# One kernel, two moved places: the last step of the projection stage, and the order of the convolution, projection and feed-forward products

## The reference, cut to what matters

```python
xn = layernorm(x)
x = x + attn(xn) + ffn(xn)

def attn(x):
    proj = x @ in_proj_w + in_proj_b             # v, ctrl 1, ctrl 2
    v = proj[..., :d]
    for i in range(2):
        ctrl = proj[..., (i + 1) * d:(i + 2) * d]
        xc = conv3(ctrl)                          # three taps along the tokens, and a bias
        gate = sigmoid(xc @ gate_w[i] + gate_b[i])
        v = long_conv(v, filter_i) * (xc * gate)
    return v @ out_proj_w + out_proj_b

def ffn(x):
    h = x @ tern_fc.T + gate * low_rank(x)
    r = maximum(h, 0)
    return (r * r) @ tern_proj.T
```

## Time and profile before

| what | value |
| --- | --- |
| median of three runs | 844.11 us (843.82 to 844.96) |
| the profiled execution's own time | 846.87 us |
| its span in the trace | 845.3 us |
| mean granted TensorE clock | 0.994 of full speed |
| PE busy | 814.5 us (96%) |
| DVE, ACT, POOL busy | 604.0 us (71%), 542.2 us (64%), 195.5 us (23%) |
| setup and projection stage | to about 312 us |
| mixing stage | about 312 to 779 us |
| output projection | about 779 us to the end |

### The profile page before, as it was taken

The page is one execution under the profiler, slowest core; times in us unless marked ns, Lnnn a source line. Parts: engine busy times, 40 slices in busy tenths (PEclk is TensorE's granted clock), DMA queues, the critical chain, the costliest instruction groups (busy, mean ns, idle before and its releaser), DMA issues.

```text
span 845.3 us, 24948 instructions
## 1 busy us (share of the span) xinstructions
PE 814.5 (96%) x9280; PEld 684.4 (81%) x9281; DVE 604.0 (71%) x992; ACT 542.2 (64%) x861; POOL 195.5 (23%) x235
## 2 busy tenths in 40 slices
PE   7899999999999979999999999999999999999997
PEld 3588888888888757788888888888888888888997
DVE  7989899999899754556565656556646656667997
ACT  6989899989989854455555555544444444444773
POOL 4944565565565000000100011000000000100000
PEclk9999999999999989999999999999999999999999
DMA  8863423422421558688868788678888877951896
GB/s 227 236 235 123 177 101 109 188 100 103 182 113 74 168 189 188 145 176 164 196 154 185 156 183 200 143 160 190 192 143 182 185 178 131 220 109 43 223 320 232
DMA packets 90541, 141.99 MB, mean 168 GB/s; under 512 B 12845, under 2 KB 70590, under 8 KB 89470
## 3 DMA queue, kind: packets, MB, share of 16 engines
q1 hardware_dynamic: 72846, 101.80, 50.3%
q0 software_dynamic: 7728, 28.05, 10.4%
q10 hardware_dynamic: 9920, 11.54, 4.1%
HBM read 97.39 MB, written 43.97 MB: 167 GB/s over the span
## 4 chain that ended last, share of the span: by engine, by line
PE 53%; DVE 5%; issue 4%; DVEq 0%
PE pp L1451 15%; PE py L1470 14%; PE pf L1420 12%; PE pf L1426 3%; PE py L1438 2%; PE py L1510 2%; DVE pp L1200 2%; DVE GC L1210 1%; DVE xb L1210 1%; PE pp L467 1%; PE pp L469 1%; PE pp L468 1%; PE pf L467 1%; PE pf L468 1%; PE pf L469 1%
## 5 line engine op out<-in xcount | busy, mean ns | idle before, releaser
L1344 ACT ACTIVATE r_hi<-r 128x512 fp32r<-128x512 f32 x128 | 80.8, 632 | 126.3 <-DVE r L1215 126.3
L1339 ACT ACTIVATE r<-pf,fscale 128x512 f32<-128x512 f32 x128 | 88.0, 688 | 103.1 <-PE pf L1426 102.1
L1470 PEld LDWEIGHTS py<-vwin,lead 64*64 64x64 f32 x5120 | 133.6, 133 | 24.6 <-issue 24.6
L1470 PE MATMUL py<-vwin,lead 64*64 64x128 f32 (+4 forms) x5120 | 147.8, 266 | 1.1 <-issue 1.1
L1420 PE MATMUL pf<-tokens,split_a 128*128 (+1 forms) x512 | 139.5, 394 | 0.7 <-issue 0.7
L1451 PE MATMUL pp<-wproj,r_hi 128*128 128x256 f32 x512 | 134.7, 296 | 4.9 <-DVE GC L1210 1.8
L1220 DVE TENSOR_TENSOR r_lo<-r,r_hi 128x512 fp32r<-128x512 f32 x128 | 88.1, 689 | 67.2 <-ACT r_hi L1344 67.1
L1451 PE MATMUL pp<-wproj,r_lo 128*128 128x256 f32 x512 | 126.9, 281 | 1.1 <-issue 1.1
L1451 PEld LDWEIGHTS pp<-wproj,r_hi 128*128 128x128 f32 x512 | 96.2, 188 | 21.9 <-issue 8.7
L508 POOL TENSOR_SCALAR lead<-lead,norms 128x256 f32<-128x256 f32 x64 | 110.2, 1732 | 3.9 <-POOL norms L502 3.4
L705 DVE SCALAR_TENSOR_TENSOR xc<-ctrls,taps,xc 128x512 f32<-128x512 f32 x128 | 96.5, 792 | 17.9 <-ACT xc L806 17.0
(11 more groups left out here) (212 smaller groups left out, 1622.6 us busy)
## 6 DMA issues: line engine op xcount, KB each, us to landing
lead<-filters SPq DMA_DIRECT2D x128, 320.0 KB, 6.2
xnT_hbm<-split_b SPq DMA_DIRECT2D x30, 512.0 KB, 3.8
tokens<-xnT_hbm POOLq DMA_DIRECT2D x30, 512.0 KB, 4.7
lead<-in_attn_x SPq DMA_DIRECT2D x16, 512.0 KB, 3.9
gc_hbm<-xc SPq DMA_DIRECT2D x16, 512.0 KB, 2.6
GC<-gc_hbm SPq DMA_DIRECT2D x32, 256.0 KB, 6.2
out<-GC ACTq DMA_DIRECT2D x15, 512.0 KB, 7.4
GC<-in_attn_x POOLq DMA_DIRECT2D x9, 512.0 KB, 7.6
```

The source lines that it names most:

```text
L1339: act.activation(r[j][:, :], pf[:, j, :], ACT.Relu, scale=fscale[:, m:m + 1]).then_inc(relu_done, 1)
L1344: act.activation(r_hi[j][:, :], r[j][:, :], ACT.Copy).then_inc(r_hi_done, 1)
L1470: last = pe.matmul(py[g % 2][q * BW:(q + 1) * BW, side, l, :, A:NB], tile[rows, q * PAIR + l, j * BW:(j + 1) * BW], vwin[g % 2][rows, q, l ...
```

## The change

It has four parts, and line numbers in the changed file differ by up to 41.

1. In step 16 ACT follows a list of its own, `last_gates`: all four first taps, then all four roundings, then all four sigmoids. The rows 2 and 3 are written to the idle control buffer `ctrl[0]` in place of `xc`, and step 16 of ACT no longer waits for `gc2_saved`. DVE's order is as before, with the new buffer. SP stores from the new buffer.
2. In step 16 PE follows `last_gates(o)`: the high-part passes for each input half as soon as that half is rounded, then the passes with the low part. The products are the same 12. The products without use are five, not seven.
3. In the mixing stage `fc(it, 2 * g)` stands ahead of `proj(*late[0])` and gives `near_mm`.
4. ACT waits for `gc2_saved` before the loop of the mixing stage; POOL loads `srow` behind the first tokens and behind a wait for `gc2_saved`.

```diff
+        def second_gates(s0):
+            return ctrl[NCH % 2][:, KT:2 * KT, 0:CH] if s0 == NCH else xc[:, KT:2 * KT, :]
+        def mixed(c, s0):
+            return xc_blocks[:, :, c, :] if c < KT else blocks(second_gates(s0)[:, c - KT, :])
...
-                    sp.dma_start(gc2_hbm[bass.ds(s - 1, 1)]..., xc[:, KT:2 * KT, :]).then_inc(gc2_saved, 16)
+                    sp.dma_start(gc2_hbm[bass.ds(s - 1, 1)]..., second_gates(s0)).then_inc(gc2_saved, 16)
...
+                def last_gates():
+                    act.wait_ge(xc_ready, 4 * s)
+                    act.wait_ge(gcT_mm, s)
+                    for c in range(4):
+                        first_tap(c)
+                    act.wait_ge(gate_mm, 4 * s)
+                    for c in range(4):
+                        high(c)
+                    for c in range(4):
+                        sigmoid(c)
+                    act.wait_ge(gcT_mm, s + 1)
+                    transposed_gates()
...
+                def last_gates(o):
+                    def passes(co, k, w, x, start=False, stop=False):
+                        c, ws = KT * o + co, slice(co * P, (co + 1) * P)
+                        return pe.matmul(pc[:, c, :], Wgate[w][:, KT * o + k, ws], xcs[o][x][:, k, :], start=start, stop=stop)
+                    for k in range(KT):
+                        pe.wait_ge(xc_hi_done, 4 * s - 4 + KT * o + k + 1)
+                        for co in range(KT):
+                            if k == 0:
+                                pe.wait_ge(gc_done, 4 * s - 4 + KT * o + co + 1)
+                            passes(co, k, 0, 0, start=k == 0)
+                            passes(co, k, 1, 0)
+                    for k in range(KT):
+                        pe.wait_ge(xc_split, 4 * s - 4 + KT * o + k + 1)
+                        for co in range(KT):
+                            last = passes(co, k, 0, 1, stop=k == KT - 1)
+                            if k == KT - 1:
+                                last.then_inc(gate_mm, 1)
...
-                    for _ in range(7):
+                    for _ in range(5):
                         pe.matmul(pT[:, 0, :], ident[:, :], Wvs[:, 0, :, :]...)
...
             pool.dma_start(bo_row[:, :], ...).then_inc(bo_in, 16)
-            pool.dma_start(srow[:, :], ...).then_inc(srow_in, 16)
             pool.wait_ge(first_in, 32)
             pool.wait_ge(y_out, 3)
             load_xn(1, 1)
+            pool.wait_ge(gc2_saved, 16 * NCH + 16)
+            pool.dma_start(srow[:, :], ...).then_inc(srow_in, 16)
             load_xb(0, True)
...
             window(0, 0, 0, 0)
             rank_high(0)
+            act.wait_ge(gc2_saved, 16 * NCH + 16)
...
+                        fc(it, 2 * g, m % 2, near_mm)
                         if late:
-                            proj(*late[0], near_mm)
-                        fc(it, 2 * g, m % 2, None if late else near_mm)
+                            proj(*late[0])
```

More of the change, by code:

```diff
@@ L704, in tap @@
                         dve.wait_ge(before, 4 * s - 4 + c + 1)
-                        dve.scalar_tensor_tensor(out=mixed(c), in0=tapped(ctrl[1 - par], c, k_), scalar=kw[:, c, k_:k_ + 1],
-                                                 in1=mixed(c), op0=ALU.mult, op1=ALU.add).then_inc(done, 1)
+                        dve.scalar_tensor_tensor(out=mixed(c, s0), in0=tapped(ctrl[1 - par], c, k_), scalar=kw[:, c, k_:k_ + 1],
+                                                 in1=mixed(c, s0), op0=ALU.mult, op1=ALU.add).then_inc(done, 1)
                 def low(c):
@@ L805, in first_tap @@
                         act.wait_ge(halo_done, 4 * s - 4 + c + 1)
-                        act.activation(mixed(c), tapped(ctrl[1 - par], c, 0), ACT.Identity, bias=kb[:, c:c + 1],
+                        act.activation(mixed(c, s0), tapped(ctrl[1 - par], c, 0), ACT.Identity, bias=kb[:, c:c + 1],
                                        scale=kw[:, c, 0:1]).then_inc(tap0_done, 1)
@@ L832, in store_V, with transposed_gates @@
                     to_V(lambda out, rows: act.activation(out, rows, ACT.Copy), act, s, s0, parity)
+                def transposed_gates():
+                    pk = (s0 - 1) % 4
+                    act.activation(GC1[:, :, bass.ds(batch(act, s - 1, s0 - 1), 1), TB * pk:TB * pk + TB].rearrange("p c n a -> p c (n a)"),
+                                   pn[:, :, :].rearrange("p i c -> p c i"), ACT.Copy).then_inc(gc1_stored, 1)
+                def last_gates():
[10 more added lines that the diff above has]
+                    transposed_gates()
+                if s0 == NCH:
+                    last_gates()
+                    return
                 if back:
@@ L931, in gates @@
                         c = KT * o + co
-                        if front:
-                            pe.wait_ge(ctrl_copied, 4 * s + c + 1)
-                        else:
-                            pe.wait_ge(gc_done, 4 * s - 4 + c + 1)
+                        pe.wait_ge(ctrl_copied, 4 * s + c + 1)
                         for k in range(KT):
@@ L945, in step @@
                     pe.wait_ge(gcT_mm, NCH)
-                    for _ in range(7):
+                    for _ in range(5):
                         pe.matmul(pT[:, 0, :], ident[:, :], Wvs[:, 0, :, :].bitcast(F32).rearrange("p k c -> p (k c)"), start=True, stop=True)
                 if back:
-                    gates(0)
+                    (gates if front else last_gates)(0)
                 if ahead and s0:
@@ L952, in step @@
                 if back:
-                    gates(1)
+                    (gates if front else last_gates)(1)
                     pe.wait_ge(gc_done, 4 * s + KT)
@@ L1157, in _ @@
             load_xn(1, 1)
+            pool.wait_ge(gc2_saved, 16 * NCH + 16)
+            pool.dma_start(srow[:, :], bass.AP(scales.tensor, 0, [[0, P], [1, D]])).then_inc(srow_in, 16)
             load_xb(0, True)
```

15 lines of the change are left out of this document (5 added, 10 removed).

## The result

The changed kernel takes **840.35 us** (median of 7 runs, 838.07 to 843.29); the kernel before, run beside it, takes 844.43 us (7 runs, 843.71 to 847.13). The ratio is 0.9943, with a 95% interval of 0.9921 to 0.9965. So it is faster, by 4.1 us where 9.4 were forecast, and 1 us above the forecast range.

A forecast was written before the change was run, and what follows sets the result against it. PE, busy for 96% of the span, was taken to bound the kernel with its products and pauses. Border 4.8 us plus mixing order 4.6 us, 9.4 in all, off 844.11 gave 834.7 us; range 832.3 to 839.4.

The forecast's parts named there:

- Taps and store: Step 16: ACT's two more taps fit its idle time, without waiting for the store; DVE goes on 2.16 us sooner.
- High passes ahead: Step 16: PE starts eight high passes at the first rounding; the 12 products run at full clock, about 1.3 and 1.5 us.
- The border, 4.8 us: Border from projection to mixing stage moves 4.8 us: 2.16 from taps, about 1.3 from passes, about 1.5 from clock.
- The clock falls at the border: Assumed at the stages' border: after a pause of about 2.5 us the first convolution still runs slow, 3.43 us.
- The likeliest case: Whole kernel: the forecast comes out as told, 834.7 us; chance 44%.
- the clock stays up: Rival, 33%: full clock over the stages' border, first convolution 2.28 us; 1.6 us more gained, 833.1 us.
- The new waits for the store: ACT's and POOL's waits for the gates' store, ahead of their mixing-stage work, cost nothing.
- `fc` ahead of `proj`, 4.6 us: Mixing stage, group 1 of fifteen passes: `proj`'s waits on `add` go and none replace them; 4.6 us gained.
- The branch: Rival, 5%: the branch on a flag shows as a pause in each group; 0.3 us a group gives 854 us.
- The sum, 9.4 us: Whole kernel: 4.8 us from the border plus 4.6 us from the mixing stage, giving 834.7 us.
- The border gives half: Rival, 8%: clock falls before step 16's 12 products, which take 4.3 us again; 836.2 to 837 us.
- the mixing stage gives nothing: Rival, 10%: the wait comes back elsewhere or filter tiles load late; only the border's gain remains, 839.3 us.

The follow-up runs named there:

- Experiment 3: Changed kernel with step 16's store from consecutive values: 840.06 us; separately, with four useless products behind the projection stage's last transposes: 841.70 us.
- experiment 5: Changed kernel with new order in group 1 alone, store from consecutive values, tokens loaded last: 838.52 us; with two useless products at the border too: 836.03 us.
- Experiment 2: Changed kernel with the load of the flag put ahead of the convolution: 846.12 us beside a kernel before of 846.29 us.
- The border part alone: Changed kernel with the old order (`proj` ahead of `fc`) in the mixing stage: 843.53 us, ratio 0.9971 to the kernel before.

## Why the prediction was right and wrong, point by point

- **Taps and store.** Right: no wait there, DVE without its pause.
- **High passes ahead, and the clock in the second gates.** Right: the gates ran at 1.00, behind a pause of 1.06 us (forecast 1.4). The store was issued at 306.24, not 306.74; 0.36 us of that is the execution's earlier start, and 0.14 is ahead of the sum.
- **The border, 4.8 us.** It gave 4.3 in this pair and 3.8 on average, since the kernel before doesn't always take 19.95 (its third trace took 18.22). The mis-sized part: the store was given 0.34 us of SP, the value for `xc`, and 1.05 us from its end to the first product. With the rows of `ctrl[0]` it takes 0.60, and the product comes 1.44 us behind it. Experiment 3 shows the 0.5 us.
- **The clock falls at the border.** The likeliest case held in this execution: the first convolution took 3.81 us. Of eleven traces with the new border and no products over the pause, it fell in eight; in three it stayed at 1.00 (behind 3.03, 3.04 and 2.53 us). So the rival "the clock stays up" came true in some executions, but its price of 1.6 us did not: in these three the second convolution starts no earlier than elsewhere, and a pause behind an instruction transfer stands ahead of it (experiment 5).
- **The new waits for the store.** Right: neither ACT's nor POOL's appears in the way.
- **`fc` ahead of `proj`, 4.6 us. This step failed**, at "so the waits go, and no later one takes their place". The named waits did go, but 0.11 us a pass came back as a slower second `proj` behind the branch, which no row names as a wait, and the other groups lost up to 0.02 us each, which the sum had as nothing. A group 1 of before was also only 0.31 us longer than its neighbours (6.93 against 6.62), and the sum took 0.34 from the first product alone. The step gives 0.14 us a pass where 0.31 was forecast; counted from the traces it is worth 2.1 to 2.5 us, by the medians 2.8 (1.0 to 4.6). Experiment 2 shows that the flag's load isn't the cause; what it is stays open.
- **The branch.** The rival of a pause in each group didn't come: in group 2 above the second `proj` follows at 0.94 us behind the first. In group 1 it follows at 0.96 us but runs 0.10 us longer. The Trainium skill (TensorE: Matmul & The Clock Gate, Part 2, Decode and dispatch) gives about 62 ns a product where the sequencer decodes it in microcode; the prediction's estimate from it has the branch hidden in every group. The trace agrees in group 2 and not quite in group 1, and no run here shows how these products are decoded.
- **The sum, 9.4 us.** The second step that failed: it has no term for what the first groups do when they begin 4 us sooner, and "no group starts its convolution late for a tile now" was read from one trace. The border part alone is 4 us shorter at the border and 2.1 us in the median. Its three traces take 41.1 us in the first groups on average against 38.9 in three of the kernel before: the right size, but the ranges overlap (38.64 to 42.60, 37.56 to 40.05). It also takes 0.9 us more to pass 9 and 0.8 in the tail than they do. The first of these repeats in all five traces with the new border and the old order, where pauses behind instruction transfers add up to 1.3 to 1.6 us, against 0.7 to 1.1 in the kernel before; with other edits of the changed kernel these two stretches come out anywhere from 21.0 to 23.7 and 84.3 to 85.8, so why the code comes later there is open. The tile waits could be removed. Behind a pause of over 3 us the granted clock fell as well, for 1.7 us more. Whether the border part meets more of all this than the kernel before does isn't settled by three traces each. The range had 0.8 us for such pauses, and only on the side of a faster result; two executions of one kernel differ by more than that.
- **The rivals.** "The border gives half", 836 to 837, had the wrong reason (the clock in the gates) but a loss of the right size. No single rival gives 840.35: both terms came out at about half at once, 4.8 as 2.1 and 4.6 as 2.8 in the medians of the parts. Of "the mixing stage gives nothing" one mishap did occur, filter tiles that come late, but in pass 0, and not in the one trace that the prediction was read from.

## What to carry to other kernels

Compare a whole group with its undisturbed neighbour, not the named waits alone: here 0.34 us of wait went and 0.18 was gained. A gain ahead of a stretch that is bound by transfers and by the first run of code isn't gained until that stretch is read too, over several executions: here its length moved by more than the edit was worth. Where engines meet, everything in the issue of the last to arrive counts, so keep the last store simple (0.5 us here). Before a gain is put down to the clock, look for what else ends the same stretch: here a fallen clock was hidden by code that came late, and a pause that no engine ended had its end in the transfers of instructions.

## What the runs showed of the hardware beyond that

- A store of two rows of 512 values a partition, with two values between them, took SP 0.60 us to issue; the same from 1024 consecutive values took 0.34.
- A load of 512 KB on POOL's queue landed in 11.8 us behind the tokens' load and in 4.5 us ahead of it.
- Behind a pause at the border of 2.5 to 3.2 us PE's granted clock fell to 0.50 in eight traces and stayed at 1.00 in three (3.03, 3.04 and 2.53 us); behind one of 1.03 or 1.13 it stayed in both. In the third trace of the kernel before it stayed behind pauses of 3.02 and 2.17 us, which is why its border took only 18.22.
- Two useless products at the border go with 2.16 us less from the first convolution to the second (6.90 against 4.74, one trace each, both at full clock). In these two traces a transfer of 16 KB of instructions began 4.26 us behind the stage's first product and 3.69 us ahead of it.
- In pass 0 PE stood still for up to 3.22 us at once with no engine named that released it, at places that changed from one execution to the next. Of 62 such pauses in 18 traces 55 end 1.3 to 1.8 us behind the end of a transfer on the instruction queue q8.
- Behind the four pauses of 3.2 to 4.0 us in pass 0 the granted clock fell, and where a convolution came right behind (three traces), it took 3.9 to 4.3 us, not 2.28.
